# Heads in 64-row array tiles, q and k laid out by way of memory off chip, x kept on chip, loops unrolled

## What is computed

```
mod = silu(c) @ wmod                      # per batch: sa, ca, ga, sb, cb, gb
h = layernorm(x) * (1 + ca) + sa
q, k, v = split(h @ W_qkv + b_qkv)        # 16 heads, d = 8
energy = einsum('bqhe,bkhe->bqhk', q, k)
attn = softmax(energy) / sqrt(128)
x = x + ga * (concat(attn @ v) @ W_out + b_out)
h = layernorm(x) * (1 + cb) + sb
x = x + gb * (quantised(h) @ quantised(weight).T + bias)   # blocks of 32, fp6 grid
```

## Time and profile before

| what | value |
|---|---|
| runs, us | 349.34, 349.99, 351.99 (median 349.99) |
| span of the profiled execution | 349.2 us |
| its own time | not listed apart from the three runs; the span lies 0.8 us under their median |
| busy: TensorE, VectorE, ScalarE, GpSimd | 304.0, 239.4, 218.5, 173.1 us |
| mean granted TensorE clock | 0.908 of full |
| DMA | 36.46 MB, 104 GB/s mean |

### The profile page before, as it was taken

The page is one execution under the profiler, slowest core; times in us unless marked ns, Lnnn a source line. Parts: engine busy times, 40 slices in busy tenths (PEclk is TensorE's granted clock), DMA queues, the critical chain, the costliest instruction groups (busy, mean ns, idle before and its releaser), DMA issues.

```text
span 349.2 us, 8125 instructions
## 1 busy us (share of the span) xinstructions
PE 304.0 (87%) x2506; PEld 216.6 (62%) x2506; DVE 239.4 (69%) x580; ACT 218.5 (63%) x404; POOL 173.1 (50%) x336
## 2 busy tenths in 40 slices
PE   3635698999899997999799997999899989999952
PEld 1204585767576765677576856677676758686521
DVE  4584587578856894779557992779677955886334
ACT  8683055876567765776477654776677645667720
POOL 4360133266736662566636672567556442546540
PEclk9955569999989998999899996999999987999995
DMA  4155365436552555345542555245544554001000
GB/s 132 32 110 115 112 178 111 113 110 174 107 132 93 159 107 122 104 154 101 112 100 94 168 116 120 90 151 103 113 126 139 107 109 126 32 19 34 18 17 15
DMA packets 23700, 36.46 MB, mean 104 GB/s; under 512 B 3422, under 2 KB 10734, under 8 KB 23670
## 3 DMA queue, kind: packets, MB, share of 16 engines
q1 hardware_dynamic: 23302, 35.43, 40.4%
q0 software_dynamic: 368, 0.66, 1.1%
HBM read 9.25 MB, written 2.13 MB: 33 GB/s over the span
## 4 chain that ended last, share of the span: by engine, by line
PE 40%; SPq 29%; DMA 16%; POOL 4%; issue 4%; DVE 3%; ACT 2%; DVEq 0%; ACTq 0%; POOLq 0%
SPq L326 24%; PE ps_o L903 10%; PE ps_p L888 9%; PE ps_p L874 8%; DMA qk_parts<-qk_parts 7%; DMA q_pad<-maxT 7%; PE ps_pre L930 3%; POOL qk_parts L371 2%; SPq L412 2%; PE ps_post L960 2%; SPq L401 2%; PE ps_o L946 1%; PE ps_post L974 1%; PE ps_post L968 1%; DMA q_pad<-qk_parts 1%
## 5 line engine op out<-in xcount | busy, mean ns | idle before, releaser
L762 DVE TENSOR_REDUCE neg_max<-ps_p 128x2 f32<-128x512 f32 x256 | 167.3, 685 | 72.7 <-PE ps_p L874 72.3
L629 ACT ACTIVATE probs<-ps_p 128x512 f32<-128x512 f32 x256 | 145.6, 595 | 82.1 <-PE ps_p L888 79.9
L874 PE MATMUL ps_p<-k_rep,q_pad 96*128 96x256 f32 x512 | 128.2, 338 | 12.1 <-DMA q_pad<-qk_parts 11.7
L888 PE MATMUL ps_p<-q_pad,k_rep 98*128 98x256 f32 x512 | 108.4, 296 | 12.5 <-DMA q_pad<-maxT 12.5
L874 PEld LDWEIGHTS ps_p<-k_rep,q_pad 96*128 96x128 f32 x512 | 84.6, 205 | 46.4 <-issue 35.0
L888 PEld LDWEIGHTS ps_p<-q_pad,k_rep 98*128 98x128 f32 x512 | 82.5, 198 | 16.8 <-issue 14.1
L903 PE MATMUL ps_o<-probs,v_aug 128*32 128x256 f32 x1024 | 82.3, 407 | 0.2 <-ACT probs L629 0.2
L903 PEld LDWEIGHTS ps_o<-probs,v_aug 128*32 128x32 f32 x1024 | 22.6, 112 | 20.2 <-issue 3.1
L530 POOL TENSOR_TENSOR wout_b<-wout_sc,modb 128x128 f32<-128x128 f32 x16 | 7.3, 459 | 49.7 <-DMA modb<-mod_rows_dram 49.6
L494 POOL CAST max_parts<-neg_max 128x16 fp32r<-128x16 f32 x32 | 6.3, 198 | 39.9 <-DVE neg_max L762 39.2
L356 POOL TENSOR_TENSOR hq<-h,rs 128x256 fp8e4<-128x256 f32 x15 | 9.3, 617 | 25.0 <-DVE rs L808 12.8
(11 more groups left out here) (107 smaller groups left out, 356.1 us busy)
## 6 DMA issues: line engine op xcount, KB each, us to landing
q_pad<-qk_parts SPq DMA_DIRECT2D x123, 64.0 KB
qk_parts<-qk_parts SPq DMA_DIRECT2D x14, 512.0 KB, 3.5
k_rep<-qk_parts SPq DMA_DIRECT2D x31, 192.0 KB
modb<-mod_rows_dram SPq DMA_DIRECT2D x16, 256.0 KB, 3.7
x_early<-in_L_attn_x_dram SPq DMA_DIRECT2D x8, 256.0 KB, 3.4
x_late<-in_L_attn_x_dram SPq DMA_DIRECT2D x8, 256.0 KB, 3.4
out_dram<-out_sb SPq DMA_DIRECT2D x16, 128.0 KB, 1.9
k_rep<-qk_parts SPq DMA_DIRECT2D x15, 128.0 KB
```

Of the source, the lines that this page charges most:

```text
L629: act.activation(probs[:, v % 2, u % 4, :], ps_p2[:, u % 2, :], ACT.Exp).then_inc(exp_done, 1)
L762: dve.tensor_reduce(neg_max[:, half, :, h % HALF], ps_p1[:, P1_BANK[h], :].rearrange("p (q k) -> p q k", q=QT), AX_X, ALU.max, negate=True ...
L874: ins = pe.matmul(ps_p1[:, P1_BANK[h], t * T:(t + 1) * T], q_pad[0:ROWS, par, h, e, t * P:(t + 1) * P], k_rep[0:ROWS, par, g, e, :], start ...
L888: ins = pe.matmul(ps_p2[:, u % 2, t * T:(t + 1) * T], k_rep[0:ROWS + 2, par, g, e, t * P:(t + 1) * P], q_pad[0:ROWS + 2, par, h, e, :], st ...
```

## The change

It does the following.

- A head's 32 rows now stand alone, without zeros: `q_rows` and `k_rows` hold 8 heads of one parity in partitions 0 to 34 and the 8 of the other parity in partitions 64 to 98. A matmul contracts over 33 rows (first scores: 32 and a row of zeros against ones) or 35 rows (second scores), in the half of the array that begins at row 0 or at row 64. In each slot the first scores use a head of one half (`P1_HEAD`) and the second scores one of the other half (`P2_HEAD`). The two matmuls of a head are issued one after the other.
- Three places (RING = 3) for laid-out pairs in place of two.
- The parts are written to a buffer in memory off chip (`parts_dram`), doubled on the way (3 DMAs for a pair), and read back into place (4 DMAs for a pair). The 22 layouts and 2 doublings go.
- x is loaded once and stays on chip (`x_all`); the per-pair loads go. The `modb` buffer has four places for two.
- A placement of maxima is two DMAs in place of one (one for each half of the array): 8 for a pair.
- The 128 x 8192 zero writes go; four DMAs on ScalarE's queue write the rows of zeros and ones at the start.
- All loops are unrolled, and all semaphore values are constants. SP's order is rewritten. The slot table of the other engines stays.

```diff
-GROUPS = [(0, 3), (3, 3), (6, 2), (8, 3), (11, 3), (14, 2)]
-ROWS = 96
-P1_BANK = [0, 1, 2, 0, 1, 0] + [2, 0, 1] * 3 + [2]
+QUAD = 4 * D
+RING = 3
+MODB_RING = 4
+P1_BANKS = 3
+P1_HEAD = [8 * (u // 8) + 2 * (u % 4) + 1 - (u % 8) // 4 for u in range(16)]
...
+    parts_dram = nc.dram_tensor("parts_dram", [NPAIR, 2, P, 4, TP], F32, kind="Internal").ap()
...
+            def store_parts(p, kind):
+                wait(sp, (low_ready, 2 * p + 1 + kind))
+                if kind == 0:
+                    src = qk_parts[:, p % 2, 0, :, :].bitcast(F32).unsqueeze(1).to_broadcast([P, 2, 2, TP])
+                    sp.dma_start(parts_dram[p, 0].rearrange("a (u v) t -> a u v t", v=2), src
+                                 ).then_inc(parts_stored[0], 16)
+                else:
+                    for part in range(2):
+                        ...
+            def lay_out(p, kind):
+                wait(sp, (parts_stored[kind], 16 * (1 + kind) * (p + 1)), (p2_full, 16 * 2 * (p - RING + 1)))
+                rows = q_rows if kind == 0 else k_rows
+                by_row = parts_dram[p, kind].rearrange("(i r d) q t -> r (d q) i t", r=2, d=D)
+                for r in range(2):
+                    dst = rows[64 * r:64 * r + QUAD, p % RING, :, :, :].rearrange("a i e t -> a i (e t)")
+                    sp.dma_start(dst.bitcast(F32), by_row[r]).then_inc(laid_out[p % RING], 16)
+            def place_max(b, half):
+                wait(sp, (maxT_saved, 2 * b + half + 1))
+                for r in range(2):
+                    sp.dma_start(q_rows[64 * r + QUAD + 1:64 * r + QUAD + 3, ...], maxT[8 * r:8 * r + 8, half, :])
...
+            store_parts(0, 0)
+            store_parts(0, 1)
+            lay_out(0, 0)
+            lay_out(0, 1)
+            sp.dma_start(x_all[:, 4:NB, :, :], x_tok[:, 4:NB]).then_inc(x_in[2], 16)
...
+            for b in range(-1, NB + 2):
+                early, late = low_pair(b), low_pair(b - 1)
+                if late is not None: lay_out(late, 1)
+                if has(b): place_max(b, 1)
+                if has(b + 1): load_modb(b + 1)
+                if has(b - 2): store(b - 2)
+                if early is not None: store_parts(early, 0)
+                if has(b + 1): place_max(b + 1, 0)
+                if early is not None: store_parts(early, 1); lay_out(early, 0)
...
+            def scores1(b, s, t):
+                h = P1_HEAD[s]
+                r, i, slot, e = h % 2, h // 2, b // 2 % RING, b % 2
+                ins = pe.matmul(ps_p1[:, (16 * b + s) % P1_BANKS, t * T:(t + 1) * T],
+                                q_rows[64 * r:64 * r + QUAD + 1, slot, i, e, t * P:(t + 1) * P],
+                                k_rows[64 * r:64 * r + QUAD + 1, slot, i, e, :], start=True, stop=True)
```

More of the change, by code:

```diff
@@ L286, in wait @@
         def wait(eng, *needs):
-            needs = [(s, n) for s, n in needs if not isinstance(n, int) or n > 0]
-            needs = [(s, n if isinstance(n, int) else eng.to_reg(n)) for s, n in needs]
             for s, n in needs:
[L292 to L299, removed]
-            wait(eng, *needs)
@@ L597, in save_hT, with save_qk @@
                                    scale=scaleT[:, col], bias=shiftT[:, col]).then_inc(hT_saved, 1)
-            def save_qk(p, par, kind, full, saved, bank=ps_pre):
-                wait(act, (full, after(p + 1, total=NPAIR)), (low_ready, after(p, 2, total=NPAIR)),
-                     *[landed(g, p - 1) for g in range(len(GROUPS))])
+            def save_qk(p, kind, full, saved, bank=ps_pre):
+                wait(act, (full, p + 1), (low_ready, 2 * p), (parts_stored[kind], 16 * (1 + kind) * (p - 1)))
@@ L848, in _ @@
-            run_pipeline(dve, pair_step)
+            for b in STEPS:
+                norm = norm_pair(b)
+                for s in range(16):
+                    if has(b + 1):
+                        maxima(b + 1, s)
+                    if s == 8 and b == -1:
+                        dve.wait_ge(const_full, 1)
+                        dve.tensor_copy(wfT[:, :], ps_p2[:, 0, 0:E])
+                        dve.tensor_tensor(attn_bias[:, :], ps_p2[:, 1, 0:E], bout_bc[:, :], ALU.add
+                                          ).then_inc(const_ready, 1)
+                    if s == 3 and has(b - 1):
+                        invert(b - 1)
+                        normalise(b - 1)
+                    if s == 3 and has(b - 2):
+                        finish(b - 2)
+                    if s == 6 and has(b - 1):
+                        residual1(b - 1)
+                    if s == 8 and has(b - 1):
+                        stats2(b - 1)
+                    if s == 4 and norm is not None and norm > 1:
+                        stats1(norm)
+                    if s == 5 and norm is not None and norm > 1:
+                        aggregate1(norm)
+                    if s == 14 and has(b - 1):
+                        if b == NB:
+                            modulate2(dve, b - 1)
+                        block_max(b - 1)
+                        block_scale(b - 1)
+                        block_inverse(b - 1)
+                        if b == NB:
+                            quantise(dve, b - 1)
@@ L893, in values, with before_scores1 @@
-            def values(b, e, v, tiles=range(QT)):
+            pe.wait_ge(wqkv_loaded, 16 * 4)
+            def before_scores1(b, s):
+                wait(pe, (max_done, 16 * b + s + 1 - P1_BANKS))
+                if s == 0 and b % 2 == 0:
+                    wait(pe, (laid_out[b // 2 % RING], 64 * (b // 2 // RING + 1)))
+            def scores1(b, s, t):
[4 more added lines that the diff above has]
+                                k_rows[64 * r:64 * r + QUAD + 1, slot, i, e, :], start=True, stop=True)
+                if t == QT - 1:
+                    ins.then_inc(p1_full, 1)
```

748 lines of the change are left out of this document (313 added, 435 removed).

## The result

The changed kernel takes 440.92 us (median of 4 runs, 426.27 to 454.62) against 350.99 for the kernel before; the ratio is 1.219, interval 1.209 to 1.230. The forecast was 326 us, range 299 to 352. The profiled execution has a span of 424.4 us, against 349.2.

The account below looks back on a forecast made before the run. Bound: TensorE's own stream, 16.8 us a step at full clock, waits adding 1.5. With -2.3, +2.0 and +0.3 a step stays 16.8; fifteen plus 2.6 low clock give 254.6 against 275.25, start -3: 326 us, range 299 to 352.

Parts of the forecast that it names:

- Placement. It no longer stands behind layouts: Sending the maxima to the second scores: two DMAs, 3.3 to 4.5 us from the transposition, 0.3 us of wait a step.
- I cost it at nothing: SP's queue: layout q waits for q's store, with layout k and the half-1 placement behind it; no cost taken.
- rival 3: The second placement comes late in every step: 1.7 us of wait in place of 0.3, 347 us; chance 0.11.
- 8 of the 11 us: TensorE's loss from work at half clock over steps 0 to 14: 8 of 11 us go, 2.6 stay at the start.
- 0.96 us of wait doesn't pull the clock down: TensorE's clock in the earlier trace: a wait of 0.96 us did not lower it; used for the placement's 0.3 us.
- Rival 3 with the clock: Late second placement and the clock falling each time too: 1.7 us more a step, 372 us; chance 0.03.
- overlap: Score matmuls in different array halves run together: three units for four in a slot, -2.3 us a step, bounds 0 and -3.8.
- Rivals 1 and 4: Row tiles do not overlap: with switches paid 356 us, chance 0.15; with switches free 326 us, chance 0.10.
- Switches: TensorE going between array shapes, 0.33 us for both sides: +2.0 us a step, bounds 0 and 2.5.
- rival 2: Shape switches are hidden and overlap is had: 15.1 us a step, 301 us; chance 0.22.
- VectorE stayed hidden: VectorE's work on the maxima is untouched at 13.5 us a step, below TensorE's 16.8, so it stays hidden.
- The start: Time up to the first second scores: at 40 to 43 us instead of 44.73, gain 3 us, bounds -2 loss, 6 gain.

Follow-up runs that it names:

- e1: Changed kernel with SP's order altered: the half-1 placement of the maxima goes ahead of the layouts; 414.0 us.
- e4: Changed kernel with the two placement DMAs issued from ScalarE's queue, right behind the copy that they read; 440.14 us.
- e5: Changed kernel with SP's order altered: the layouts split and spread over the pair, with the placements between; 370.13 us.
- e6: Changed kernel, its order kept, with each score tile widened to 62 or 64 rows by rows of zeros; 382.81 us.
- e2: Changed kernel with the first scores taken from the same half of the array as the slot's second scores, so nothing overlaps; 587.34 us.
- e8: Changed kernel with zero-filled 62/64-row tiles and both scores of a slot from the same half of the array; 516.17 us.
- e10: Changed kernel with layouts spread, zero-filled 62/64-row tiles, and only the first pair's buffers filled ahead of the modulation; 336.75 us, ratio 0.957.
- e9: Changed kernel with layouts spread and full-array scores over rows 0:97 or 0:99, leaving out the separation of a pair's heads; 341.3 us.
- e11: Changed kernel with ScalarE's exponential of c ahead of its four DMAs of constants; 421.42 us.
- e12: Kernel before the change, with its half-0 placement moved ahead of the store and the two layouts; 336.74 us, ratio 0.959.

## Why the prediction was wrong

**The step that failed** is "Placement. It no longer stands behind layouts", with its twin on SP, "I cost it at nothing". The half-1 placement stands behind both layouts. I had read the order and noted it for SP's own time, where the round trip is indeed cheap: SP issued the placement at 154.71, soon enough. I priced the queue by when SP issues and took 1.9 to 3.1 us to landing from the earlier trace rows; in the 3.13 us of the earlier trace rows the DMA engines' share was 0.51. With 2 MB in one block they are full for 14 us, and it took 9.2. I also took DMA traffic to fall: the DMAs are fewer, but they move 44.20 MB for 36.46. The bytes were in the text (2 MB, 4 to 6 us for its landing), and weren't laid under the placement. Forecast 0.3 us a step, measured 33.8 in 15: 2.3. e1, e4 and e5 show the cause from three sides. This term alone, 2 us a step more than forecast, makes the 326 into about 355 us (rival 3, with 1.7 a step, had 347).

**The step that cost most** is the clock, which the sum holds at 2.6 us. I took the return to full clock from before (a few us) and let "8 of the 11 us" go. The new matmuls have each a third of the rows at work and no longer bring it back in that time: about +54 us in place of -8, the largest term of all. e6 (zeros added, 46 us less than the changed kernel), e2 and e8 show that it is the rows of the tiles and not the waits alone. The waits start the falls, but they needn't be long: in e5 one came after 0.39 and 0.36 us, and in e1 the clock, down since the start, stayed down to 143 us with waits of 2.06 and 2.22 us in between. My sentence that 0.96 us of wait doesn't pull the clock down holds for the 98-row matmuls of before; in e5 0.66 and 0.95 us were followed by a long dip, in e10 (62/64 rows) six waits of 0.6 to 1.0 us were followed by none. Why the rows matter is not shown.

**Rival 3 with the clock**, 372 us and a chance of 0.03, was the right mechanism at under half of its size: it gave 25 us of low clock, 1.7 a step, where some 65 were lost, mostly behind 8 waits.

**Right or nearly:** overlap. Forecast three units for four in a slot (-2.3 a step, bound -3.8), measured two in most slots, near the bound; the order in which they start was not the one that I took. Rivals 1 and 4 fall. Switches are paid, so rival 2 falls: with -3.8 at most from overlap and 0.8 net in e10 against e9, they cost up to 3.0 us a step by difference, above the 2.0 taken and perhaps above its bound of 2.5; no run measures them alone. Net -0.8 where I had -0.3: the two errors partly cancel, which is luck. VectorE stayed hidden, and SP idle: right, and worth nothing. The chance for faster by over 1% is a slip of the sum: the four terms give 0.77, not 0.78.

**The start:** forecast -3 us, bounds -6 to +2, measured +11.3. I gave ScalarE's four issues about 2.5 us; they took 7.8, and the exponential's table load (1.28 us) stood behind them (with the exponential first, e11, 7.8 of the 11.3 are gone). The k layout lands 11 us after its issue, not 4 to 6.

**What the change could bring:** e10 against e12, 336.75 and 336.74 us: nothing beyond what one moved transfer gives the kernel before. The gain of the mended tiles over full-array scores is a quarter of a microsecond a step, as the freed time turns into waits for DMAs.

## What to carry to other kernels

Before a small, urgent transfer is moved, lay the bytes issued just ahead of it under it, on the DMA engines and not only on the queue: megabytes that nobody waits for can hold 8 KB that everybody waits for. Before matmuls are made thinner, look at what TensorE's clock does after a wait; rows of zeros cost no time here (32.84 us for two steps with 33/35 and with 62/64 rows) and brought the clock back sooner. And try the order of transfers in the old kernel first: one moved call was worth 4%.

## What the runs showed of the hardware that I had not expected

- TensorE at 0.50 for over 500 us while busy without gaps, in same-half tiles of 33/35 rows (e2); 62/64 rows with zeros: 0.644 (e8).
- Return to full clock after a wait of 4 to 5.5 us: 13 to 32 us with 33/35-row tiles in two halves, 5 to 9 with 62/64, 5 to 16 with 97/99 rows over the whole array, without halves.
- A step at the half level (0.50) kept TensorE busy 1.6 times as long as at full clock, not twice (24.21 and 14.81 us, e1 and e5).
- Matmuls given out A0 A1 B0 B1, A and B in different halves, start in pairs A0 B0 and A1 B1, 0.01 us apart.
- An 8 KB DMA from another queue still waits behind 2 MB in part (e4: longest wait 4.2 us); the second DMA of 144 KB of ones into three partitions held its issuing engine for 4.79 us, the first for 0.83.
